# Expert layers of a recurrent and mixture-of-experts kernel: alternating one by one, or in pairs with four activation buffers

## The chip, the cores and the metric

The kernel runs on one core of a Trainium2 chip. The metric is the device time of one execution in microseconds (us); the time before is 6597.48 us, the median of three runs.

## The reference

Input `x` is [4, 4096, 512], float32 throughout. After a layer norm `xn`, two branches meet:

```python
# branch 1, a recurrence over every second token (2048 steps), state h [4, 512, 64]
xz = rms_norm(xn[:, ::2]) @ w_in.T + b_in ; x_proj, gate = split(xz)
h = tanh(h * A + x_t[:, :, None] * Bm)           # one step
y = h @ c_sum + Dv * x_t
s = repeat((y * silu(gate)) @ w_out.T + b_out, 2)
# branch 2, a mixture of experts over every token: H=1024, M=64, E=8, EH=512, top 2
cont = sigmoid(xn @ W_enc + b_enc) @ W_s2c + b_s2c            # [tokens, 64]
probs = softmax(cont @ Wr + br); gate = top-2 weights, normalised, zero elsewhere
hid = relu(cont @ W1[e] + b1[e]) ; y_e = hid @ W2[e] + b2[e]  # for each of 8 experts
decoded = sigmoid((sum_e gate_e * y_e) @ W_c2s + b_c2s) @ W_dec + b_dec
out = x + s * silu(layer_norm(decoded))
```

## The kernel before

The sequence is cut into 64 blocks of 32 recurrence steps (64 tokens of each of 4 batches, 256 tokens a block). All 8 experts are computed for all tokens; the gate scales their input (`conte`, cont times gate, with the gate itself as a 65th row that carries the bias), so that their outputs simply add up in PSUM.

**The recurrence** is done in `step` and `tanh`: 128 partitions hold batch and half of the states, two halves `f` lie in the free dimension. In a step GpSimd (POOL) makes `u = x * Bm` (L499), VectorE (DVE) two products `ps_z = h * A` (L991) and two sums `ps_z += u` (L997), ScalarE (ACT) two tanh (L601). `u` has two buffers: POOL may be one step ahead. Every four steps TensorE (PE) reads `h` for `y` (L761); `h` is a ring of 8 steps, so tanh of step 20 waits for the `y` of steps 12 to 15.

**Everything else** is hung between the steps by hand. The tables at the top give each piece a slot, counted in steps of its block: `ACT_RELU = (13.5, 13.5, 14.5, 14.5, 15.5, ...)` means that ACT does the first two ReLUs after the first tanh of step 13. Negative slots are in the block before, slots of 32 and more in the block after. Each engine runs its own list in order; semaphores join them. Each engine's program is: block 0, a loop of 31 rounds with two blocks each, block 63.

What PE does in a block, in its order, from the experts on:

- `experts` rounds 0 to 16. Round n does `expert_up(n)` (L845: two matmuls of 65 rows and 128 columns of weights over 256 tokens into `bank[n % 2]`, the two halves of one PSUM bank) and then `expert_down(n - 1)` (L857: two matmuls with 64 columns of weights, into the lower and upper half of `ps_acc`). ACT's `relu(n)` (L682) lies between: it takes the bank to `hT[:, n % 2]`. Up n waits until relu n - 2 has freed the bank, down n until relu n is there. The biases of the second layer are one matmul (L853) before the first down. Two calls of `y` are laid between.
- `to_spikes` (L879), `y`, `decode` (L900, two times 8 matmuls of 512 columns, and a one-row bias matmul L892 each), `y`, `encode` of the next block (L794), two `y` and one more.
- `controller` (L806, 64-column weights, result `contT` in `ps_acc`), `fin_transpose` (L912), `router`, `fin_out` (L919 and L921) for the block before, the transposes of the next input (L772), `proj_in` (L781), `y`, the transposes of `conte` (L833), and then the experts.

`router` does, for each of two halves of the tokens, three matmuls: the bias row `br` (one row, L815), cont times `w_r` with 8 columns (L816), and cont times an identity with 64 columns, which transposes it (L817). `logits_copy` (L651), `route` on DVE and `scale_cont` (L665) read them in `ps_acc`.

Around it: DVE's `dec_stats` (L1061) waits for decode, `fin_mul` (L1098, L1099) for `fin_out`; POOL's `fin_skip` (L551) writes into `o`, which is the first part of `conte`'s memory.

Of the kernel before, what the change touches and what calls it, by code (L numbers as in the profile page):

```python
# [23 lines left out]
ACT = mybir.ActivationFunctionType  # L24
AX = mybir.AxisListType

P = 128
# [12 lines left out]
KH = H // P  # L40
M = 64
MA = M + 1
E = 8
EH = 512
T2 = 2 * P
# [6 lines left out]
FILL_ENC, FILL_FIN, FILL_XT, FILL_WIN, FILL_CONTE, FILL_W1, FILL_C2S, FILL_DEC = 0, 4, 6, 8, 10, 14, 30, 33  # L52
# [36 lines left out]
PE_ROUTER = 8  # L89
PE_CONTET = (17, 17, 18, 18)  # L90
PE_GATET = 18
PE_EXPERTS = (19, 19, 19, 19, 19, 19, 19, 19, 19, 19, 19, 20, 22, 22, 24, 28, 28)
PE_TO_SPIKES = (31, 31, 31, 31)
PE_DECODE = (33, 33)
PE_FIN_TRANSPOSE = 39
# [14 lines left out]
def build(nc, x, w_inT, b_in, A_T, B_T, Cm, Dv, w_outT, b_out, g_norm, W_enc, b_enc, W_s2c, b_s2c,  # L110
# [12 lines left out]
    with ExitStack() as ctx:  # L123
        def sb(name, shape):
            return ctx.enter_context(nc.sbuf_tensor(name, shape, F32))
# [9 lines left out]
        w_out = sb("w_out", [P, KD, D])  # L135
        w_enc = sb("w_enc", [P, KD, H])
        w_s2c = sb("w_s2c", [P, KH, M])
        w_r = sb("w_r", [P, E])
        w_1 = sb("w_1", [P, E, EH])
        w_2 = sb("w_2", [P, E * EH // P, M])  # L140
        w_c2s = sb("w_c2s", [P, H])
# [2 lines left out]
        bias_rows = sb("bias_rows", [P, D])  # L144
        ones = sb("ones", [P, P])
# [6 lines left out]
        g_col = sb("g_col", [P, KD])  # L152
        cont_bias = sb("cont_bias", [P, 1])
        ident = sb("ident", [P, P])
        ident_2 = sb("ident_2", [P, M])
        before = sb("before", [P, E, E])
        c_wide = sb("c_wide", [P, F, 2 * SP - 4])
        minus_half = sb("minus_half", [P, 2])
# [15 lines left out]
        hT = sb("hT", [P, 2, 2 * T2])  # L174
# [15 lines left out]
        eoT = hT[:, 0, 0:T2]  # L190
        contT = hT[:, 1, 0:T2]
        gateT = w_1[96:96 + E, 0, 0:T2]
        bias_2 = w_1[96:96 + E, 1, 0:M]
        conteT = wide[0:MA, :, :].rearrange("p (e) t -> p e t", e=E)
        conte_flat = conte[:, :, :, :].rearrange("p q e m -> p (q e m)")
        o = conte_flat[:, 0:D]
        oT = conte_flat[:, D:2 * D].rearrange("p (k t) -> p k t", k=KD)


        ps_A = pb("ps_A", [P, F, D])  # L200
# [2 lines left out]
        bank = [pb("bank0", [P, D]), pb("bank1", [P, D])]  # L203
        ps_acc = pb("ps_acc", [P, D])
        eo_acc = ps_acc[:, 0:T2]
        contT_acc = ps_acc[:, 0:T2]
        gateT_acc = ps_acc[0:E, 0:T2]
        cont_acc = ps_acc[:, T2:T2 + 2 * M].rearrange("p (q m) -> p q m", q=2)
        L0 = T2 + 2 * M
        logit_acc = ps_acc[:, L0:L0 + 2 * E].rearrange("p (q e) -> p q e", q=2)  # L210

        atleast = ps_acc[:, 0:2 * E * E].rearrange("p (q e j) -> p q e j", q=2, e=E)
        rank = ps_acc[:, 128:144].rearrange("p (q e) -> p q e", q=2)
# [40 lines left out]
        eo_ready = sem("eo_ready")  # L254
# [44 lines left out]
        def wait_filled(eng, at):  # L299
            eng.wait_ge(bank_filled[at[1] % 2], count_of(at))  # L300
# [13 lines left out]
        def drained(ins, at):  # L314
            ins.then_inc(bank_drained[at[1] % 2], 1)
# [10 lines left out]
        def wait_dec_drained(eng, blk, q):  # L326
            if q == 0:
                wait_drained(eng, (blk, FILL_DEC))
            else:
                eng.wait_ge(acc_drained, 2 * blk + 2)  # L330
# [42 lines left out]
        def _(sp):  # L373
            def load(dst, src):
                sp.dma_start(dst, src).then_inc(weights_loaded, 16)  # L375
                n_loads[0] += 1
# [54 lines left out]
            load(w_s2c[:, :, :], W_s2c.rearrange("(k p) n -> p k n", p=P))  # L431
            load(bias_rows[0:1, :], b_dec.partition_broadcast(1))
            load(bias_rows[32:33, :], b_out.partition_broadcast(1))
            load(bias_rows[64:65, 0:E], br.partition_broadcast(1))
            load(cont_bias[0:M, :], b_s2c)
            for half in range(2):
                load(w_r[M * half:M * half + M, :], Wr)
            load(w_1[0:M, :, :], W1.rearrange("e m h -> m e h"))
            load(w_1[M:MA, :, :].rearrange("p e h -> p (e h)"), b1.rearrange("e h -> (e h)").partition_broadcast(1))
            load(w_2[:, :, :], W2.rearrange("e (t p) m -> p (e t) m", p=P))  # L440
# [35 lines left out]
        def _(pool):  # L476
# [70 lines left out]
            def fin_skip(blk, par):  # L547


                wait_filled(pool, (blk, FILL_CONTE + 3))  # L550
                pool.tensor_tensor(o, xp[:, par, :], dv_all[:, :], ALU.mult).then_inc(t1_ready, 1)  # L551

            def fin_gate(blk, par):
# [38 lines left out]
        def _(act):  # L592
# [86 lines left out]
            def relu(blk, n):  # L679
                at = (blk, FILL_W1 + n)  # L680
                wait_filled(act, at)
                drained(act.activation(hT[:, n % 2, :], bank[n % 2][:, :], ACT.Relu), at)  # L682

            def eo_copy(blk):
                act.wait_ge(eo_ready, blk + 1)
# [13 lines left out]
            act.wait_ge(pool_made, 8)  # L699
            for half in range(2):  # L700
                rows = slice(M * half, M * half + M)
                act.activation(ident_2[rows, :], ident[rows, rows], ACT.Copy)
            act.activation(ps_A[:, 0, :], h[:, 0, 0, :], ACT.Copy)
            act.activation(ps_A[:, 1, :], h[:, 0, 1, :], ACT.Copy).then_inc(ready, 1)
            proj_norm(0)
# [47 lines left out]
        def _(pe):  # L753
# [44 lines left out]
            def controller(blk):  # L798

                wait_drained(pe, (blk, FILL_ENC + 2))  # L800
                wait_drained(pe, (blk, FILL_ENC + 3))
                if not is_first(blk):
                    wait_dec_drained(pe, blk - 1, 1)
                for k in range(KH):
                    half = k % 2
                    ins = pe.matmul(contT_acc[M * half:M * half + M, :], w_s2c[:, k, :], wide[:, k, :],  # L806
                                    start=(k < 2), stop=(k >= KH - 2))
                ins.then_inc(contT_ready, 1)

            def router(blk):  # L810

                pe.wait_ge(contT_copied, blk + 1)
                for q in range(2):
                    tokens = contT[:, P * q:P * q + P]
                    pe.matmul(logit_acc[:, q, :], ones[64:65, :], bias_rows[64:65, 0:E], start=True, stop=False)  # L815
                    pe.matmul(logit_acc[:, q, :], tokens, w_r[:, :], start=False, stop=True)  # L816
                    ins = pe.matmul(cont_acc[:, q, :], tokens, ident_2[:, :], start=True, stop=True)  # L817
                ins.then_inc(logits_ready, 1)

            def gateT_transpose(blk):  # L820
# [15 lines left out]
            def expert_up(blk, n):  # L836

                at = (blk, FILL_W1 + n)
                e = n // 2
                if n % 4 == 0:  # L840
                    wait_drained(pe, (blk, FILL_CONTE + n // 4))
                wait_free(pe, at)
                for half in range(2):
                    t = 2 * (n % 2) + half
                    ins = pe.matmul(bank[n % 2][:, T2 * half:T2 * half + T2], w_1[0:MA, e, P * t:P * t + P],  # L845
                                    conteT[:, e, :], start=True, stop=True)
                filled(ins, at)

            def expert_down(blk, n):

                if n == 0:
                    pe.wait_ge(gateT_copied, blk + 1)
                    pe.matmul(eo_acc[0:M, :], bias_2, gateT, start=True, stop=False)  # L853
                wait_drained(pe, (blk, FILL_W1 + n))
                for half in range(2):
                    t = 2 * (n % 2) + half
                    ins = pe.matmul(eo_acc[M * half:M * half + M, :], w_2[:, 4 * (n // 2) + t, :],  # L857
                                    hT[:, n % 2, T2 * half:T2 * half + T2],
                                    start=(n == 0 and half == 1), stop=(n == 15))
                if n == 15:  # L860
                    ins.then_inc(eo_ready, 1)

            def experts(blk, n):

                if n < 16:
                    expert_up(blk, n)
                if n > 0:
                    expert_down(blk, n - 1)

            def to_spikes(blk, n):  # L870
                if n == 0:
# [69 lines left out]
            def between(blk, par, slot):  # L941
                for k in range(NQ):
                    if slot == PE_Y[k]:
                        y(blk, k)
                for q in range(2):
                    if slot == PE_PROJ_TRANSPOSE[q]:
                        proj_transpose(blk, q)
                for half in range(2):
                    if slot == PE_PROJ_IN[half]:
                        proj_in(blk, par, half)  # L950
                for n in range(4):
                    if slot == PE_ENCODE[n]:
                        encode(blk, par, n)
                if slot == PE_CONTROLLER:
                    controller(blk)
                if slot == PE_ROUTER:
                    router(blk)
                for n in range(4):
                    if slot == PE_CONTET[n]:
                        conteT_transpose(blk, n)  # L960
                if slot == PE_GATET:
                    gateT_transpose(blk)
                for n in range(17):
                    if slot == PE_EXPERTS[n]:
                        experts(blk, n)
                for n in range(4):
                    if slot == PE_TO_SPIKES[n]:
                        to_spikes(blk, n)
                for q in range(2):
                    if slot == PE_DECODE[q]:  # L970
                        decode(blk, q)
                if slot == PE_FIN_TRANSPOSE:
                    fin_transpose(blk)
                if slot == PE_FIN_OUT:
                    fin_out(blk)
# [5 lines left out]
        def _(dve):  # L981
# [121 lines left out]
            dve.memset(ones[:, :], 1.0)  # L1103
            dve.memset(c_wide[:, :, :], 0.0)
            dve.memset(h[:, RING - 1, :, :], 0.0)
            dve.memset(cont_bias[M:P, :], 0.0).then_inc(consts_made, 1)
            dve.wait_ge(consts_made, 1)
            proj_stats(0)
# [76 lines left out]
```

## Time and profile before

| | us |
|---|---|
| median of 3 runs (6596.17 to 6603.51) | 6597.48 |
| profiled execution, span | 6604.5 |
| PE busy (matmuls) | 6237.1 |
| DVE busy | 5737.4 |
| POOL busy | 5612.7 |
| ACT busy | 3984.4 |

The profile lists an execution of its own; its span is 7.0 us above the median. Busy time of PE has matmuls with modelled ends, so a busy PE may be waiting inside. PEld is the loading of weights, which overlaps. A float32 matmul call stands as two instructions in the trace: x4 in a row is two calls. "issue" means that nothing in the profile explains the wait.

### The profile page before, as it was taken

What the parts mean: (1) busy time and instruction counts of PE and PEld (TensorE: products, weight loads), DVE (VectorE), ACT (ScalarE), POOL (GpSimd) and SP (SyncE); (2) the same over time, 40 slices, a digit from 0 to 9 for tenths busy, and PEclk for the clock granted to TensorE, in tenths of its full rate; (3) what the DMA queues carried; (4) which work ended last, traced back from release to release, by engine and by line L of the source; (5) the groups of instructions that cost most, each with busy time, mean ns of one, the idle gap of its engine ahead of it and who ended that gap; (6) DMA issues with size and microseconds to landing.
All of it is one profiled execution on the core that took longest, in us unless ns stands there. A gap on an engine that the chain in (4) does not pass through costs nothing.

```text
span 6604.5 us, 111352 instructions
## 1 busy us (share of the span) xinstructions
PE 6237.1 (94%) x29376; PEld 3229.9 (49%) x29376; DVE 5737.4 (87%) x10060; ACT 3984.4 (60%) x8390; POOL 5612.7 (85%) x3276
## 2 busy tenths in 40 slices
PE   5999999999999999999999999999999999999998
PEld 3554445445544454454444544445444545444454
DVE  4988889888898888988888888889888898888887
ACT  3666566566565665656656656566566665565665
POOL 4888888888888888888888888888888888888887
PEclk9999999999999999999999999999999999999999
DMA  5443444444444444444344444444444444434443
GB/s 138 104 108 92 104 109 98 106 101 101 105 98 102 100 97 106 103 97 110 93 105 101 100 106 98 103 106 96 105 101 100 106 98 103 106 95 105 103 100 83
DMA packets 158032, 675.52 MB, mean 102 GB/s; under 512 B 45589, under 2 KB 46613, under 8 KB 91799
## 3 DMA queue, kind: packets, MB, share of 16 engines
q1 hardware_dynamic: 157336, 667.24, 41.6%
q8 instruction: 315, 5.16, 0.3%
q14 instruction: 381, 3.12, 0.2%
HBM read 616.73 MB, written 50.33 MB: 101 GB/s over the span
## 4 chain that ended last, share of the span: by engine, by line
POOL 54%; issue 29%; PE 13%; DVE 1%; POOLq 1%; SPq 1%; ACT 1%; DMA 0%; DVEq 0%; ACTq 0%
POOL u L499 46%; PE bank L845 3%; POOL g L545 2%; PE ps_y L761 2%; PE ps_acc L857 2%; PE bank L794 1%; PE bank L781 1%; POOL gt L532 1%; POOL d_r L541 1%; PE bank L900 1%; PE ps_acc L900 1%; POOL conte L551 1%; PE bank L921 1%; POOL p_r L515 1%; SPq L375 1%
## 5 line engine op out<-in xcount | busy, mean ns | idle before, releaser
L499 POOL TENSOR_TENSOR u<-xb,bt 128x1024 f32<-128x1024 f32 x2048 | 4832.9, 2366 | 789.2 <-DVE ps_z L997 782.8
L601 ACT ACTIVATE h<-ps_z 128x512 f32<-128x512 f32 x4096 | 2374.7, 601 | 1691.8 <-DVE ps_z L997 1587.5
L991 DVE TENSOR_TENSOR ps_z<-h,ps_A 128x512 f32<-128x512 f32 x4096 | 2674.1, 691 | 517.3 <-ACT h L601 329.2
L997 DVE TENSOR_TENSOR ps_z<-ps_z,u 128x512 f32<-128x512 f32 x4096 | 2660.7, 691 | 39.6 <-POOL u L499 37.3
L845 PE MATMUL bank<-wide,w 65*128 65x256 f32 x4096 | 1141.2, 404 | 1.9
L761 PE MATMUL ps_y<-h,c_wide 128*32 128x512 f32 x8192 | 1007.1, 610 | 80.4 <-ACT h L601 80.4
L794 PE MATMUL bank<-xnT,w_enc 128*128 128x256 f32 x4096 | 922.4, 384 | 49.5 <-DVE g L1082 42.6
L845 PEld LDWEIGHTS bank<-wide,w 65*128 65x128 f32 x4096 | 700.2, 189 | 449.8 <-issue 320.2
L794 PEld LDWEIGHTS bank<-xnT,w_enc 128*128 128x128 f32 x4096 | 772.4, 191 | 256.9 <-issue 81.0
L682 ACT ACTIVATE hT<-bank 128x512 f32<-128x512 f32 x1024 | 604.0, 598 | 383.8 <-PE bank L845 366.4
L857 PE MATMUL ps_acc<-hT,w 128*64 128x256 f32 x4096 | 668.7, 405 | 6.6
L761 PEld LDWEIGHTS ps_y<-h,c_wide 128*32 128x32 f32 x8192 | 216.3, 110 | 615.2 <-issue 416.3
L900 PE MATMUL bank<-w_dec,wide 128*128 128x512 f32 x1024 | 480.3, 624 | 0.0
L900 PE MATMUL ps_acc<-w_dec,wide 128*128 128x512 f32 x1024 | 456.6, 599 | 0.0
L781 PE MATMUL bank<-w_in,xnT 128*128 128x512 f32 x1024 | 453.9, 597 | 0.0
L857 PEld LDWEIGHTS ps_acc<-hT,w 128*64 128x64 f32 x4096 | 202.5, 134 | 357.2 <-issue 296.8
L900 PEld LDWEIGHTS bank<-w_dec,wide 128*128 128x128 f32 x1024 | 199.1, 200 | 286.4 <-issue 286.4
L900 PEld LDWEIGHTS ps_acc<-w_dec,wide 128*128 128x128 f32 x1024 | 189.7, 190 | 262.4 <-issue 262.4
L921 PE MATMUL bank<-w_out,conte 128*128 128x512 f32 x512 | 313.9, 770 | 0.0
L624 ACT ACTIVATE wide<-bank,b_enc_col 128x256 f32<-128x256 f32 x512 | 213.9, 471 | 148.1 <-PE bank L794 148.1
L781 PEld LDWEIGHTS bank<-w_in,xnT 128*128 128x128 f32 x1024 | 191.4, 192 | 216.8 <-issue 216.5
L665 ACT ACTIVATE conte<-ps_acc,gate 128x64 f32<-128x64 f32 x1024 | 226.5, 369 | 0.0
(107 smaller groups left out, 4324.6 us busy)
## 6 DMA issues: line engine op xcount, KB each, us to landing
xb<-x_proj_scratch SPq DMA_DIRECT2D x2048, 256.0 KB, 4.3
xbuf<-in_L_attn_x SPq DMA_DIRECT2D x256, 128.0 KB
xres<-in_L_attn_x SPq DMA_DIRECT2D x512, 64.0 KB
out<-g SPq DMA_DIRECT2D x256, 128.0 KB
x_proj_scratch<-xp SPq DMA_DIRECT2D x256, 64.0 KB
w_in<-in_L_attn_w_in SPq DMA_DIRECT2D x1, 2048.0 KB
w_enc<-in_L_ffn_W_enc SPq DMA_DIRECT2D x1, 2048.0 KB
w_dec<-in_L_ffn_W_dec SPq DMA_DIRECT2D x1, 2048.0 KB
```

Source lines behind the costliest of these rows:

```text
L499: pool.tensor_tensor(u[:, tau % 2, :, :], xt, bt[:, :, :], ALU.mult).then_inc(u_ready, 1)
L601: act.activation(h[:, tau % RING, f, :], ps_z[:, f, :], ACT.Tanh).then_inc(h_ready, 1)
L682: drained(act.activation(hT[:, n % 2, :], bank[n % 2][:, :], ACT.Relu), at)
L761: ins = pe.matmul(ps_y[32 * j:32 * j + 32, :], c_wide[:, f, SP - 4 - 4 * k:2 * SP - 4 - 4 * k], h[:, (QUAD * k + j) % RING, f, :], start=( ...
L781: ins = pe.matmul(bank[half][:, :], xnT[:, par, k, 0, :], w_in[:, k, D * half:D * half + D], start=(k == 0), stop=(k == KD - 1))
L794: ins = pe.matmul(bank[n % 2][:, T2 * half:T2 * half + T2], w_enc[:, k, P * m:P * m + P], xnT[:, par, k, :, :], start=(k == 0), stop=(k == ...
L845: ins = pe.matmul(bank[n % 2][:, T2 * half:T2 * half + T2], w_1[0:MA, e, P * t:P * t + P], conteT[:, e, :], start=True, stop=True)
L857: ins = pe.matmul(eo_acc[M * half:M * half + M, :], w_2[:, 4 * (n // 2) + t, :], hT[:, n % 2, T2 * half:T2 * half + T2], start=(n == 0 and ...
L900: ins = pe.matmul(dst[:, :], wide[:, k, P * q:P * q + P], w_dec[:, k, :], start=False, stop=(k == KH - 1))
L921: ins = pe.matmul(bank[1][:, :], oT[:, k, :], w_out[:, k, :], start=False, stop=(k == KD - 1))
L991: dve.tensor_tensor(ps_z[:, f, :], h[:, (tau - 1) % RING, f, :], ps_A[:, f, :], ALU.mult).then_inc(m_done, 1)
L997: dve.tensor_tensor(ps_z[:, f, :], ps_z[:, f, :], u[:, tau % 2, f, :], ALU.add).then_inc(z_ready, 1)
```

## The change

- Experts go in pairs: nine rounds, round p does up 2p, up 2p + 1, then down 2p - 2, down 2p - 1. `PE_EXPERTS` has nine slots. ReLU results have four places: the two of `hT`, and two in `conte`'s memory, which nothing reads once it is transposed. ACT's slots are the same.
- POOL's `fin_skip`, which writes into that memory, waits until the last down is done (`eo_ready`) and no longer for the last transpose of `conte`.
- The router has one matmul for each half of the tokens, 72 columns wide: `w_r` and the identity lie side by side. The bias of both halves (144 columns, one row) is put into `ps_acc` by one matmul ahead of the controller's; this one opens the bank, the others accumulate.

```diff
-PE_EXPERTS = (19, 19, 19, 19, 19, 19, 19, 19, 19, 19, 19, 20, 22, 22, 24, 28, 28)
+PE_EXPERTS = (19, 19, 19, 19, 19, 20, 22, 24, 28)
...
-        w_r = sb("w_r", [P, E])
+        w_r = sb("w_r", [P, E + M])
...
+        br_row = w_1[96:97, 2, 0:2 * (E + M)]
...
+        hidden = [hT[:, 0, :], hT[:, 1, :], conte_flat[:, 0:2 * T2], conte_flat[:, 2 * T2:4 * T2]]
...
+        routed = ps_acc[:, T2:T2 + 2 * (E + M)].rearrange("p (q n) -> p q n", q=2)
+        logit_acc = routed[:, :, 0:E]
+        cont_acc = routed[:, :, E:E + M]
...
-                wait_filled(pool, (blk, FILL_CONTE + 3))
+                pool.wait_ge(eo_ready, blk + 1)
...
-                drained(act.activation(hT[:, n % 2, :], bank[n % 2][:, :], ACT.Relu), at)
+                drained(act.activation(hidden[n % 4], bank[n % 2][:, :], ACT.Relu), at)
...
+                pe.matmul(ps_acc[:, T2:T2 + 2 * (E + M)], ones[96:97, :], br_row, start=True, stop=True)
                 for k in range(KH):
                     half = k % 2
                     ins = pe.matmul(contT_acc[M * half:M * half + M, :], w_s2c[:, k, :], wide[:, k, :],
-                                    start=(k < 2), stop=(k >= KH - 2))
+                                    start=False, stop=(k >= KH - 2), skip_group_check=True)
...
-                    pe.matmul(logit_acc[:, q, :], ones[64:65, :], bias_rows[64:65, 0:E], start=True, stop=False)
-                    pe.matmul(logit_acc[:, q, :], tokens, w_r[:, :], start=False, stop=True)
-                    ins = pe.matmul(cont_acc[:, q, :], tokens, ident_2[:, :], start=True, stop=True)
+                    ins = pe.matmul(routed[:, q, :], tokens, w_r[:, :], start=False, stop=True,
+                                    skip_group_check=True)
...
-                                    hT[:, n % 2, T2 * half:T2 * half + T2],
+                                    hidden[n % 4][:, T2 * half:T2 * half + T2],
...
-            def experts(blk, n):
+            def experts(blk, p):
 
-                if n < 16:
-                    expert_up(blk, n)
-                if n > 0:
-                    expert_down(blk, n - 1)
+                if p < 8:
+                    expert_up(blk, 2 * p)
+                    expert_up(blk, 2 * p + 1)
+                if p > 0:
+                    expert_down(blk, 2 * p - 2)
+                    expert_down(blk, 2 * p - 1)
```

PE at the start of the experts, in the loop, before (`wide` holds the transposed `conte`, `w` is `w_1` or `w_2`):

```order
L845 MATMUL bank<-wide,w 128x256 x4
L853 MATMUL ps_acc<-w 64x256
L303 REGISTER_ALU
L857 MATMUL ps_acc<-hT,w 64x256 x2
L845 MATMUL bank<-wide,w 128x256 x2
L857 MATMUL ps_acc<-hT,w 64x256 x2
L845 MATMUL bank<-wide,w 128x256 x2
```

and in the change:

```order
L848 MATMUL bank<-wide,w 128x256 x4
L310 REGISTER_ALU
L848 MATMUL bank<-wide,w 128x256 x4
L856 MATMUL ps_acc<-w 64x256
L860 MATMUL ps_acc<-hT,w 64x256 x4
L310 REGISTER_ALU
L848 MATMUL bank<-wide,w 128x256 x4
L860 MATMUL ps_acc<-conte,w 64x256 x4
```

A run of ups or downs is now twice as long; the first down comes after four ups and no longer after two.

PE around the router, in the loop, before:

```order
L806 MATMUL ps_acc<-wide,w_s2c 64x256 x8
L912 MATMUL bank<-ident,conte 128x128 x4
L812 REGISTER_ALU
L815 MATMUL ps_acc<-bias_rows,ones 128x8
L816 MATMUL ps_acc<-w_r,hT 128x8
L817 MATMUL ps_acc<-ident,hT 128x64
L815 MATMUL ps_acc<-bias_rows,ones 128x8
L816 MATMUL ps_acc<-w_r,hT 128x8
L817 MATMUL ps_acc<-ident,hT 128x64
L303 REGISTER_ALU
L919 MATMUL bank<-bias_rows,ones 128x512
```

and in the change:

```order
L807 MATMUL ps_acc<-w,ones 128x144
L810 MATMUL ps_acc<-wide,w_s2c 64x256 x8
L917 MATMUL bank<-ident,conte 128x128 x4
L816 REGISTER_ALU
L819 MATMUL ps_acc<-w_r,hT 128x72 x2
L304 REGISTER_ALU
L924 MATMUL bank<-bias_rows,ones 128x512
```

Six small calls have become two, and one call with a single row stands ahead of the controller.

## Rows read from the trace of the kernel before

**Rows 1.** The profile's page, part 1: busy us, share, instructions.
```profile
PE 6237.1 (94%) x29376; PEld 3229.9 (49%) x29376; DVE 5737.4 (87%) x10060; ACT 3984.4 (60%) x8390; POOL 5612.7 (85%) x3276
```

**Rows 2.** Line L686, once a block: ns min/median/max, first and last start.
```profile
L686 ACT ACTIVATE hT<-ps_acc x64: 404/405/408, 155.5 to 6552.7; 128x256 f32<-128x256 f32 x64
```

**Rows 3.** Timeline of PE, experts of one block: start, length (us), times, idle before.
```profile
3070.99 2.00 PE L845 MATMUL bank<-wide,w 65*128 65x256 f32 x8
3072.91 0.64 PE L853 MATMUL ps_acc<-w 8*64 8x256 f32 x2
3073.49 0.65 PE L857 MATMUL ps_acc<-hT,w 128*64 128x256 f32 x4
3074.07 1.13 PE L845 MATMUL bank<-wide,w 65*128 65x256 f32 x4
3075.13 0.65 PE L857 MATMUL ps_acc<-hT,w 128*64 128x256 f32 x4
...
3098.35 1.41 PE L857 MATMUL ps_acc<-hT,w 128*64 128x256 f32 x8
3099.68 1.92 PE L761 MATMUL ps_y<-h,c_wide 128*32 128x512 f32 x16
```

**Rows 4.** Timeline of ACT, experts of that block.
```profile
3080.17 0.60 ACT L682 ACTIVATE hT<-bank 128x512 f32<-128x512 f32 x1 [1.05 <-PE bank L845]
3080.66 1.08 ACT L601 ACTIVATE h<-ps_z 128x512 f32<-128x512 f32 x2
3081.81 0.60 ACT L682 ACTIVATE hT<-bank 128x512 f32<-128x512 f32 x1
```

**Rows 5.** Timeline of DVE: two steps among the experts, two after them.
```profile
3081.28 1.29 DVE L991 TENSOR_TENSOR ps_z<-h,ps_A 128x512 f32<-128x512 f32 x2 [0.79 <-ACT h L601]
3084.57 1.29 DVE L991 TENSOR_TENSOR ps_z<-h,ps_A 128x512 f32<-128x512 f32 x2 [0.79 <-ACT h L601]
...
3104.77 1.29 DVE L991 TENSOR_TENSOR ps_z<-h,ps_A 128x512 f32<-128x512 f32 x2
3107.32 1.29 DVE L991 TENSOR_TENSOR ps_z<-h,ps_A 128x512 f32<-128x512 f32 x2
```

**Rows 6.** Busy time by stretch: length, PE, PEld, DVE, ACT, POOL, granted clock, DMA.
```profile
3080.00:3101.00 21.00, 20.90 (x118) 9.99 (x120) 16.98 (x28) 14.01 (x26) 17.22 (x8) 1.00 0.28 66
3101.00:3143.00 42.00, 42.00 (x188) 23.17 (x180) 40.67 (x68) 24.22 (x48) 40.30 (x24) 1.00 0.54 137
...
3149.60:3153.00 3.40, 3.40 (x5) 1.33 (x4) 2.86 (x8) 2.65 (x5) 3.40 (x3) 0.50 0.49 104
```

**Rows 7.** Timeline of all engines around the router.
```profile
3143.05 1.95 PE L806 MATMUL ps_acc<-wide,w_s2c 128*64 128x256 f32 x16
3145.57 0.38 PE L815 MATMUL ps_acc<-bias_rows,ones 1*128 1x8 f32 x2
3145.88 0.39 PE L816 MATMUL ps_acc<-w_r,hT 128*128 128x8 f32 x2
3145.89 0.60 ACT L696 ACTIVATE conte<-bank 128x512 f32<-128x512 f32 x1
3146.12 0.41 PE L817 MATMUL ps_acc<-ident,hT 128*128 128x64 f32 x2
3147.37 1.12 PE L919 MATMUL bank<-bias_rows,ones 1*128 1x512 f32 x2
3151.48 1.27 POOL L545 TENSOR_TENSOR g<-g,sg 128x512 f32<-128x512 f32 x1
3153.95 0.69 DVE L1098 TENSOR_TENSOR g<-bank,g 128x512 f32<-128x512 f32 x1 [1.46 <-PE bank L921]
```

**Rows 8.** Timeline, the next block, where the loop's round ends.
```profile
3205.48 1.93 PE L761 MATMUL ps_y<-h,c_wide 128*32 128x512 f32 x16 [2.33 <-ACT h L601]
3228.97 1.29 DVE L991 TENSOR_TENSOR ps_z<-h,ps_A 128x512 f32<-128x512 f32 x2 [4.12 <-issue]
```

**Rows 9.** Spans and granted clock.
```profile
core 0: 6604.5 us, clock 0.975
```

More of the change, by code:

```diff
@@ L154, in build @@
         ident = sb("ident", [P, P])
-        ident_2 = sb("ident_2", [P, M])
         before = sb("before", [P, E, E])
@@ L207, in build @@
         gateT_acc = ps_acc[0:E, 0:T2]
-        cont_acc = ps_acc[:, T2:T2 + 2 * M].rearrange("p (q m) -> p q m", q=2)
-        L0 = T2 + 2 * M
-        logit_acc = ps_acc[:, L0:L0 + 2 * E].rearrange("p (q e) -> p q e", q=2)
+        routed = ps_acc[:, T2:T2 + 2 * (E + M)].rearrange("p (q n) -> p q n", q=2)
+        logit_acc = routed[:, :, 0:E]
+        cont_acc = routed[:, :, E:E + M]
         atleast = ps_acc[:, 0:2 * E * E].rearrange("p (q e j) -> p q e j", q=2, e=E)
@@ L433, in _ @@
             load(bias_rows[32:33, :], b_out.partition_broadcast(1))
-            load(bias_rows[64:65, 0:E], br.partition_broadcast(1))
+            for q in range(2):
+                load(br_row[:, (E + M) * q:(E + M) * q + E], br.partition_broadcast(1))
             load(cont_bias[0:M, :], b_s2c)
             for half in range(2):
-                load(w_r[M * half:M * half + M, :], Wr)
+                load(w_r[M * half:M * half + M, 0:E], Wr)
             load(w_1[0:M, :, :], W1.rearrange("e m h -> m e h"))
@@ L701, in _ @@
                 rows = slice(M * half, M * half + M)
-                act.activation(ident_2[rows, :], ident[rows, rows], ACT.Copy)
+                act.activation(w_r[rows, E:E + M], ident[rows, rows], ACT.Copy)
             act.activation(ps_A[:, 0, :], h[:, 0, 0, :], ACT.Copy)
@@ L962, in between @@
                     gateT_transpose(blk)
-                for n in range(17):
+                for n in range(9):
                     if slot == PE_EXPERTS[n]:
@@ L1105, in _ @@
             dve.memset(h[:, RING - 1, :, :], 0.0)
+            for q in range(2):
+                dve.memset(br_row[:, (E + M) * q + E:(E + M) * (q + 1)], 0.0)
             dve.memset(cont_bias[M:P, :], 0.0).then_inc(consts_made, 1)
```

## The prediction

> **What bounds the kernel now.** I read the page's busy times first, then one block in the timelines, engine by engine. PE is busy 94% of the span, DVE 87%, POOL 85% [rows 1], so three engines could bound it and only the waits in a block can tell which does where. One line that runs once a block starts first at 155.5 and last at 6552.7, 64 times [rows 2]: 6397.2 / 63 = 101.5 us a block. What a block saves is saved 64 times.
>
> The stretches of one block show two kinds of time [rows 6]. From 3080 to 3101, among the experts, PE is busy 20.90 of 21.00, while DVE is busy 16.98 and POOL 17.22: **PE leads here**, and the others idle some 4 us. How they hang on it is seen in ACT's and DVE's rows. ACT's ReLU waits 1.05 for the up matmul, and only behind it comes the next tanh [rows 4]; DVE's products wait 0.79 for that tanh, and one step follows the other after 84.57 - 81.28 = 3.29 us, against 107.32 - 104.77 = 2.55 after the experts [rows 5]. 3.29 is two expert rounds of PE: an up takes 3075.13 - 3074.07 = 1.06 and a down 3074.07 - 3073.49 = 0.58, so a round takes 1.64 [rows 3].
>
> From 3101 to 3143 PE is busy 42.00 of 42.00, DVE 40.67 and POOL 40.30 [rows 6]: all three are nearly full. Nothing in the change shortens this stretch; it can only begin earlier. Then comes the router's stretch, in which DVE's `fin_mul` waits 1.46 for `fin_out` [rows 7], partly because PE runs at a granted clock of 0.50, the 1.2 GHz level, from 3149.6 to 3153.0 [rows 6]. At the end of a loop round DVE stands 4.12 and PE 2.33 [rows 8]; it is the loop's branch, the change leaves it alone, and it falls on every second block.
>
> **The experts in pairs.** Before, PE needs 3099.68 - 3070.99 = 28.69 us from the first up to the second `y` [rows 3]. It adds up: two ups in a row 1.92, bias 0.58, 14 single ups at 1.06, 14 single downs at 0.58, the last two downs 1.33 (they wait for a ReLU), one `y` of 1.86 (its 1.92 less the overlap), together 28.65. What a repeated shape costs stands in two rows. Two ups in a row are 2.00 long and one is 1.13, so the second costs 0.87 and not 1.06 [rows 3]. Four pairs of 64-column matmuls side by side, the controller's, are 1.95 long [rows 7], and one such pair, a down, is 0.65 [rows 3]: each further pair costs 0.43 and not 0.58. So a change of shape from up to down and back costs 0.19 + 0.15 = 0.34 us, and the change takes away about half of these.
>
> After: 8 double ups at 1.92 are 15.36, 8 double downs at 0.58 + 0.43 = 1.01 are 8.08, bias 0.58, `y` 1.86: 25.88. That is **2.81 less a block**. The double down is what no row shows undisturbed. Its bounds: 1.01 as above, and 1.33, the only two downs in a row [rows 3], with which the gain is 28.69 - (15.36 + 10.64 + 0.58 + 1.86) = 0.25. I take 1.01, since the controller's matmuls have the same shape (128 rows, 64 columns, 256 tokens) and no ReLU between them.
>
> Do the others follow? A group of two ups and two downs takes 1.92 + 1.01 = 2.93 us, still above the 2.55 that a step needs without waits, so PE keeps the lead and DVE gains with it. ACT has two ReLUs and two tanh in it, 0.60 + 0.60 + 1.08 = 2.3 us [rows 4], which fits. The first ReLU of a group can start about 1 us after the ups begin, and its bank is needed again after 2.93, so a pair of tanh (1.08) can come in between with some 0.3 us to spare; the four places free the second ReLU from waiting for a down. DVE's and POOL's idle 4 us among the experts hold 2.8. The tanh of step 20, which waits for the first `y` in this stretch, gets it earlier too, since six groups lie ahead of it instead of twelve rounds.
>
> **The router.** Six calls take 3147.37 - 3145.57 = 1.80, 0.30 each; two remain, 0.60. The new one-row call ahead of the controller is bounded by the one-row call with 8 columns, 0.31 from start to start, and the bias row of `fin_out` with 512, 1.12 long [rows 7]; by columns it lies at about 0.5. I take 0.5. So PE would save 0.7. But `fin_out` also waits for ACT's L696, which starts at 3145.89 and lasts 0.60; it moves back by the same 0.5 with the controller, to 3146.99, so `fin_out` starts at about 3147.04 instead of 3147.37: 0.33 us. Behind it POOL's L545 ends at 3152.75, and `fin_mul` needs it; so at most 3153.95 - 3152.75 = 1.2 us can be gained here, even with a full clock [rows 7]. Where PE isn't late (blocks with full clock here), the gain is 0. I take 0.2 a block, with 0 and 1.2 as ends. The ACT copy of `contT` and the tanh behind it come 0.5 later; DVE is then busy with two other instructions, so I cost this at nothing; without that cover it would be up to 0.5 a block.
>
> **Smaller parts.** POOL's `fin_skip` stands in slot 31, some 20 us after the last down: the new wait costs nothing. ACT, DVE, POOL and SP have the same instructions in the loop. The setup has two small loads and two memsets more, under the large weight loads: nothing.
>
> **Sum.** 2.8 + 0.2 = 3.0 us a block, 64 blocks: 192. The profiled execution spans 6604.5, so 6412; its span lies 7 above the median, so **6405 us**.
>
> **Rivals.**
> 1. *Half of it is lost.* ReLUs come in pairs right behind a double up, and a tanh pair comes between them; if each group waits 0.2 us for ACT, a block loses 8 x 0.2 = 1.6, and the time is 6405 + 102 = 6507. For it speaks the narrow margin of 0.3 us above, and that DVE, POOL and PE are all nearly full after the experts, so that a gain must reach all three; against it, that ACT is idle 7.0 of 21.0 us in this stretch [rows 6].
> 2. *Repeating a shape saves nothing.* The 0.19 and 0.15 belong to the loading of weights and not to the change of shape; they would show in every call. Then only the router is left, 0.2 x 64 = 13 us: about 6585, and with the ACT delay of the router uncovered 6597. The rows speak against it: the second of two ups is cheaper by 0.19, though its weights are loaded too. The Trainium skill (TensorE: Matmul & The Clock Gate, Part 3, "What overlaps and what doesn't") says that weights load beside a running matmul only when the row group differs; up and down both use all row groups here, so by it grouping would bring nothing. The trace disagrees so far, by that second up of 0.87.
> 3. *Slower: PE's clock.* The mean granted clock is 0.975 [rows 9], so some 5% of the span, 330 us, are at 1.2 GHz, 5.2 us a block. They come after stretches in which PE had small calls (the router) or stood at the loop's end [rows 6, 8]. With a shorter program PE waits more often for DVE; if the low clock came to cover `decode` in every block, each us at 1.2 GHz costs half a us. To eat 3.0 us a block it needs 6.0 us more of it, more than twice as much as now; with 8 us more the time is 6405 + 64 x 4 = 6661. Against it: the change removes small calls and puts in no wait where PE leads. The Trainium skill (same page, "Why this matters for your kernels") warns of idle gaps between bursts of matmuls; here PE has one gap of 2.33 in two blocks, as before.
>
> **How the numbers follow.** About 0.2% is what a measurement of this kernel can tell from no change, 13 us. The forecast, 6350 to 6465, has 0.73; rival 1 (6465 to 6584) 0.18; rival 2 0.05; rival 3 0.04. Faster 0.91, same 0.05, slower 0.04. The low end is reached with 2.8 + 1.2 a block, 256 us: 6341; the high end with half of the experts' gain, 1.4 a block: 6508. The clock may shift either by some 30 us. I give 6345 to 6505.
>
> **What would show it.** In the profile after: double ups start to start 1.92 and double downs 1.01; from first up to second `y` 25.9 instead of 28.7; steps among the experts 2.93 apart; L686 98.5 apart on average. The router's two calls take 0.6, the new bias call 0.5. I am wrong if groups take 3.3 (rival 2), if PE rows among the experts show waits for ACT (rival 1), or if the mean clock falls below 0.95 (rival 3).

## The result, and the profile after

The change is slower: 6787.2 us median of 4 runs (6752.29 to 6834.85) against 6598.35, a ratio of 1.0288 with a 95% interval of 1.0244 to 1.0332. The forecast was 6405, faster. Of `pairs_only` and `start_then_singles` further down, two of four executions each ran over 1.5% above the fastest of the same kernel, and their times and ratios below leave these out. PE's new rows came out as forecast and the time did not, so the clock is the first thing to look at. Three lines of the page of the changed kernel (the span, the busy times, the granted clock in 40 slices), and its mean clock:

```profile
span 6833.1 us, 110339 instructions
...
PE 6389.3 (94%) x28992; PEld 3440.5 (50%) x28992; DVE 5740.9 (84%) x10062; ACT 3987.0 (58%) x8390; POOL 5613.7 (82%) x3276
...
PEclk9998889998899899899799998898989999989988
```

```profile
core 0: 6833.1 us, clock 0.919
```

PE is busy 152 us longer than in [rows 1], with 384 instructions fewer, and the mean granted clock fell from 0.975 [rows 9] to 0.919. The trace shows where: in 28 of 64 blocks it falls to 0.50, the 1.2 GHz level, 3.1 to 5.4 us after the first up (the first matmul of the experts), and it is back only 24 to 31 us later, 806 us in all. Before the change it never fell there. One such block by stretches (columns as in [rows 6]):

```profile
690.00:731.00 41.00, 38.59 (x188) 21.70 (x190) 40.15 (x78) 25.07 (x62) 39.63 (x30) 1.00 0.46 109
731.00:739.10 8.10, 7.58 (x53) 4.37 (x46) 7.50 (x13) 6.60 (x13) 6.85 (x3) 1.00 0.31 66
739.10:769.80 30.70, 30.70 (x96) 16.17 (x94) 15.71 (x26) 11.95 (x22) 17.93 (x9) 0.50 0.30 69
```

In the last one PE is busy 30.70 of 30.70 us and still gets 1.2 GHz, while DVE is busy only half of the time. The timeline of PE there, which answers to [rows 3]:

```profile
735.88 1.99 PE L848 MATMUL bank<-wide,w 65*128 65x256 f32 x8
738.36 3.08 PE L848 MATMUL bank<-wide,w 65*128 65x256 f32 x8 [0.49 <-ACT hT L684]
741.37 1.11 PE L856 MATMUL ps_acc<-w 8*64 8x256 f32 x2
742.41 1.98 PE L860 MATMUL ps_acc<-hT,w 128*64 128x256 f32 x8
744.31 3.78 PE L848 MATMUL bank<-wide,w 65*128 65x256 f32 x8
748.02 1.97 PE L860 MATMUL ps_acc<-conte,w 128*64 128x256 f32 x8
...
766.78 3.41 PE L763 MATMUL ps_y<-h,c_wide 128*32 128x512 f32 x16
770.12 1.99 PE L848 MATMUL bank<-wide,w 65*128 65x256 f32 x8
```

A double up is 1.99 long at full clock and 3.78 at the low one. Two things were not in the forecast. PE **stands still for 0.49 us before the third up**, and the low clock holds until `y` (L763) comes. Why it stands still is in ACT's timeline:

```profile
736.73 1.09 ACT L603 ACTIVATE h<-ps_z 128x512 f32<-128x512 f32 x2
737.70 1.09 ACT L684 ACTIVATE hT<-bank 128x512 f32<-128x512 f32 x2
```

The third up needs the bank that ReLU 0 frees. ReLU 0 has its slot behind the second tanh of step 13 (slot 13.5 means that, and not behind the first tanh, as the section on the kernel before has it). It starts at 737.70 and ends about 738.3; PE goes on at 738.36. Before the change ReLU 0 came at the same place, 1.82 us after the first up of [rows 3]:

```profile
3071.84 1.09 ACT L601 ACTIVATE h<-ps_z 128x512 f32<-128x512 f32 x2
3072.81 1.10 ACT L682 ACTIVATE hT<-bank 128x512 f32<-128x512 f32 x2
```

It ended about 3073.4, while the bias matmul ran from 3072.91; the first down followed at 3073.49 and the third up at 3074.07, so no wait was seen.

### The profile page after: what moved, and what is told of

Same layout as the page of the kernel before. It is cut to its first block, busy times and chain, and to the rows that moved or that the text cites. A ratio compares the mean times of both kernels' runs of the same rounds, so it can differ in the third digit from the quotient of the medians.

```text
span 6833.1 us, 110339 instructions
## 1 busy us (share of the span) xinstructions
PE 6389.3 (94%) x28992; PEld 3440.5 (50%) x28992; DVE 5740.9 (84%) x10062; ACT 3987.0 (58%) x8390; POOL 5613.7 (82%) x3276
## 4 chain that ended last, share of the span: by engine, by line
POOL 51%; issue 31%; PE 13%; DVE 2%; ACT 2%; POOLq 1%; SPq 1%; DMA 0%; DVEq 0%; ACTq 0%
POOL u L501 43%; PE bank L848 3%; PE ps_y L763 2%; POOL g L547 2%; PE ps_acc L860 2%; PE bank L783 2%; POOL gt L534 1%; DVE ps_z L1002 1%; ACT h L603 1%; PE bank L796 1%; POOL d_r L543 1%; POOL conte L553 1%; DVE ps_z L996 1%; POOL g L566 1%; POOL conte L557 1%
## 5 line engine op out<-in xcount | busy, mean ns | idle before, releaser
L848 PE MATMUL bank<-wide,w 65*128 65x256 f32 x4096 | 1235.4, 453 | 33.0 <-ACT hT L684 31.0
L763 PE MATMUL ps_y<-h,c_wide 128*32 128x512 f32 x8192 | 1035.8, 625 | 93.8 <-ACT h L603 93.8
L848 PEld LDWEIGHTS bank<-wide,w 65*128 65x128 f32 x4096 | 864.3, 222 | 438.3 <-issue 234.9
L763 PEld LDWEIGHTS ps_y<-h,c_wide 128*32 128x32 f32 x8192 | 219.9, 112 | 655.7 <-issue 453.8
L783 PE MATMUL bank<-w_in,xnT 128*128 128x512 f32 x1024 | 479.3, 623 | 0.0
L684 ACT ACTIVATE hT<-bank 128x512 f32<-128x512 f32 x512 | 299.7, 601 | 260.9 <-PE bank L848 260.9
L684 ACT ACTIVATE conte<-bank 128x512 f32<-128x512 f32 x512 | 292.6, 597 | 213.1 <-PE bank L848 209.4
L860 PE MATMUL ps_acc<-hT,w 128*64 128x256 f32 x2048 | 349.6, 473 | 0.0
L860 PE MATMUL ps_acc<-conte,w 128*64 128x256 f32 x2048 | 324.1, 444 | 0.0
L926 PE MATMUL bank<-w_out,conte 128*128 128x512 f32 x512 | 268.4, 673 | 0.0
```

The costliest lines, as they stand in the source:

```text
L684: drained(act.activation(hidden[n % 4], bank[n % 2][:, :], ACT.Relu), at)
L763: ins = pe.matmul(ps_y[32 * j:32 * j + 32, :], c_wide[:, f, SP - 4 - 4 * k:2 * SP - 4 - 4 * k], h[:, (QUAD * k + j) % RING, f, :], start=( ...
L783: ins = pe.matmul(bank[half][:, :], xnT[:, par, k, 0, :], w_in[:, k, D * half:D * half + D], start=(k == 0), stop=(k == KD - 1))
L926: ins = pe.matmul(bank[1][:, :], oT[:, k, :], w_out[:, k, :], start=False, stop=(k == KD - 1))
```

## The experiments

Three theories for the falls: (A) the start with four ups in a row causes them; (B) pairs anywhere do; (C) the router's part does. A was later split in two: (A1) the standstill, or four ups with nothing between them; (A2) the late first down. A fourth, (D), came later too: the clock falls, and stays low, because ups use only 65 of the 128 rows of the array. "Falls" below means falls of the clock among the experts, counted in one profiled execution of 64 blocks. Times are medians, and ratios are to the kernel before, run on the same chip, where it took 6606 to 6610 us.

**pairs_only** and **router_only**: each half of the change alone.

> Experts in pairs, router as before. Seen after the change: in 27 of 64 blocks the granted clock falls to 0.5 some 3 to 5 us after the first up and stays there for 27 to 31 us. If the pairs cause it (theory A: the start with four ups; theory B: pairs anywhere), the time stays near that of the change, 6740 to 6860, mean clock about 0.92, with falls among the experts. If the router's part causes it (theory C, by shifting where low activity falls), the time is near 6420 and the clock 0.97.

> Router with one matmul per half, experts one by one as before. Theories A and B: 6575 to 6600 (the 0 to 0.33 us a block of the prediction), no fall of the clock among the experts. Theory C: 6700 or more, falls among the experts.

`pairs_only` took 6786 us (ratio 1.0267, 1.0235 to 1.0299) with 23 falls; `router_only` 6566.16 (0.9937, 0.9918 to 0.9957) with none. Theory C is out. The router's part is a gain by itself, 0.6%, and more than I expected (6575 to 6600). By the medians it is 40 us, 0.63 us a block, about three times the 0.2 that I took for it; by the interval of the ratio 0.4 to 0.85. The clock goes with it: the four executions run from 6556.58 at a mean clock of 0.982 to 6584.32 at 0.977. In the profiled one, the fastest, the low stretches from the controller's first matmul to the next block's first up sum to 133 us; in the profile before they sum to 181.

**start_then_singles** and **singles_then_pairs**: the order of the experts, written out (u is up, d down, b the bias).

```diff
-PE_EXPERTS = (19, 19, 19, 19, 19, 20, 22, 24, 28)
+# start_then_singles
+EXPERT_ROUNDS = ('u0 u1', 'u2 u3 b d0 d1', 'u4 d2', 'u5 d3', ..., 'u15 d13', 'd14 d15')
+# singles_then_pairs
+EXPERT_ROUNDS = ('u0', 'u1 b d0', 'u2 d1', 'u3 d2', 'u4 u5 d3', 'u6 u7 d4 d5', ..., 'u14 u15 d12 d13', 'd14 d15')
```

> The change, but only its first four ups in a row; after the first two downs ups and downs alternate one by one. Theory A (the start makes the clock fall): falls 3 to 5 us after the first up as in the change; how long they last tells whether alternating gets the clock back (short, about 10 us) or whether nothing in the experts does (27 us and more, up to the next y). Theory B (pairs anywhere): falls gone or at another place, 6590 to 6620. Theory A gives 6700 to 6900.

> The change, but ups 0 to 3 and downs 0 to 2 one by one as before, pairs from up 4 on. Theory A: no fall among the experts, since the start is as before; six of eight groups keep the gain of 0.34 us each, some 2 us a block: 6440 to 6500. Theory B: falls later among the experts, 6600 to 6850.

`start_then_singles` took 6845 us (1.0356, 1.0324 to 1.0388), within theory A's range. The execution that was profiled took 7013.97 and has 30 falls at the same place, 3.1 to 5.5 us after the first up. The two executions behind the 6845 have mean clocks of 0.937 and 0.932, which fits falls there too, fewer of them. So the start is enough. And alternating does not get the clock back: the falls last 27 to 34 us, up to `y`. One such block of that profile, the low stretch and what follows:

```profile
2027.80:2058.50 30.70, 30.70 (x87) 14.30 (x90) 15.53 (x25) 12.07 (x22) 16.49 (x9) 0.50 0.31 69
2058.50:2068.90 10.40, 10.40 (x68) 4.61 (x60) 7.12 (x12) 5.92 (x12) 5.97 (x3) 1.00 0.16 45
```

`singles_then_pairs` took 6497.72 us (0.9827, 0.9811 to 0.9843), no falls. Theory A holds, B is out: six double ups kept the full clock in all 64 blocks.

**What in the start it is.** Three edits of the change:

```diff
+# bias_between
+EXPERT_ROUNDS = ('u0 u1', 'b u2 u3 d0 d1', 'u4 u5 d2 d3', ..., 'd14 d15')
+# relu_earlier
-ACT_RELU = (13.5, 13.5, 14.5, ...)
+ACT_RELU = (13, 13.5, 14.5, ...)
+# two_singles
+EXPERT_ROUNDS = ('u0', 'u1 b d0', 'u2 u3 d1', 'u4 u5 d2 d3', ..., 'd14 d15')
```

> The change, with the bias matmul (0.58 us) between the second and the third up instead of behind the fourth. In the change PE stands still 0.49 us there, waiting for the first ReLU. Theory A1 (it is the standstill, or four 65-row ups with nothing between): no falls of the clock among the experts, 6400 to 6470. Theory A2 (it is how late the first down comes, still behind four ups, 4.4 us after the first): falls in about as many blocks as after the change, 6740 to 6860.

> The change, with the first ReLU before the second tanh of step 13 instead of behind it. The order on PE is that of the change, only the standstill before the third up shrinks from 0.49 to 0.1 us or less. Theory A1, by the standstill alone: no falls, 6400 to 6470. Theory A2, or if four ups in a row are enough by themselves: falls stay, 6730 to 6850.

> The change, with up 0, up 1, bias, down 0 as before, and pairs right from up 2. The first 4 us then hold four ups and two downs instead of four ups. Theory A2: few or no falls, and up to 0.7 us a block more than with three single rounds: 6440 to 6500. If falls come back here (6600 or more), two single rounds are too few and the stretch that matters is longer.

`relu_earlier` took 6449.48 us (0.9755, 0.9736 to 0.9775), no falls. PE does the same instructions in the same order as after the change; the standstill is down to 0.07 us (the third up starts 1.99 us after the first, where a double up takes 1.92; in the change 2.48):

```profile
3094.13 4.10 PE L848 MATMUL bank<-wide,w 65*128 65x256 f32 x16
3098.16 0.64 PE L856 MATMUL ps_acc<-w 8*64 8x256 f32 x2
3098.73 1.08 PE L860 MATMUL ps_acc<-hT,w 128*64 128x256 f32 x8
3099.75 1.99 PE L848 MATMUL bank<-wide,w 65*128 65x256 f32 x8
...
3120.09 1.92 PE L763 MATMUL ps_y<-h,c_wide 128*32 128x512 f32 x16
```

So four ups in a row are not enough by themselves: **in this order of PE the clock falls in 28 of 64 blocks with the 0.49 us of standstill, and in none without it**. `bias_between` took 6485.09 us (0.9809, 0.9761 to 0.9857; two executions, 6458.49 and 6511.69, at mean clocks of 0.970 and 0.960). It has no standstill either, but a matmul of 8 rows and 64 columns in its place, and 9 falls are left of the 28. That is neither of my two expectations: falls come without a standstill too, if a small matmul stands there, though fewer. `two_singles` took 6451.91 (0.9759, 0.9739 to 0.9778), no falls: the bias and one down of 128 rows before the third up are enough. Its time fell in the range of theory A2, but `relu_earlier`, where the first down is as late as in the change, rules A2 out as the cause by itself.

**rows128**: the same start, standstill included, but more of the array at work. The 63 rows that are added have zero weights; the data under them are not zero, they are what `wide` still holds of the encoder's sigmoid. The small tables that lay in these rows of `w_1` have a tile of their own (not shown).

```diff
-                    ins = pe.matmul(bank[n % 2][...], w_1[0:MA, e, P * t:P * t + P], conteT[:, e, :], ...)
+                    ins = pe.matmul(bank[n % 2][...], w_1[:, e, P * t:P * t + P], conteT_all[:, e, :], ...)
+            dve.memset(w_1[M:P, :, :], 0.0).then_inc(w_1_cleared, 1)
```

> The change, with all ups over 128 rows instead of 65: the 63 rows added have zero weights, so the result is the same and each matmul takes the same time; the small tables that lay in the unused rows have a tile of their own. Theory D (what lets the clock fall, and keeps it low for 27 us and more although PE is never idle, is that ups use only half of the rows): no falls, or short ones; 6390 to 6470. If rows do not matter, falls as after the change, 6740 to 6860.

6505.3 us (0.9838, 0.9804 to 0.9873), and no falls. The standstill is there, the durations are the same:

```profile
2418.60 1.99 PE L852 MATMUL bank<-wide,w 128*128 128x256 f32 x8
2421.08 1.99 PE L852 MATMUL bank<-wide,w 128*128 128x256 f32 x8 [0.49 <-ACT hT L688]
```

The falls are gone as theory D has it, but the time lies above my range of 6390 to 6470. That range was made with the forecast's 3.0 us a block, and `relu_earlier` shows that 2.5 were to be had; the rest of the miss stays open (see the next section).

**rows128_late**: 65 rows in ups 0 to 3, 128 from up 4 on (`w_1[0:P if n > 3 else MA, ...]`). This lets the falls come and asks how long they last.

> The change with ups 0 to 3 over 65 rows as in it, and ups 4 to 15 over 128 rows (63 of them with zero weights). The start, and so the falls of the clock 3 to 5 us after the first up, should be those of the change (in 20 to 30 of 64 blocks). If the clock then stays low because ups with half of the rows are too little for it to rise (theory D), it comes back within some 3 to 10 us instead of 27 to 31, and the time is 6500 to 6620. If rows play no part in that, it stays low up to the y behind six groups, 27 us, and the time is 6700 or more.

6561.57 us (0.9926, 0.9906 to 0.9946). 27 falls, at 3.1 to 5.5 us as after the change, but each lasts 3.4 or 6.8 us, and 109 us in all instead of 806. One of them, by stretches and in PE's timeline:

```profile
2137.00:2140.40 3.40, 3.40 (x12) 1.99 (x9) 3.34 (x7) 1.60 (x3) 3.21 (x2) 0.50 0.95 217
2140.40:2160.00 19.60, 19.60 (x121) 11.81 (x123) 15.71 (x26) 13.91 (x26) 15.89 (x9) 1.00 0.25 57
```

```profile
2134.31 1.99 PE L852 MATMUL bank<-wide,w 65*128 65x256 f32 x8 [0.48 <-ACT hT L688]
2136.23 0.64 PE L860 MATMUL ps_acc<-extra 8*64 8x256 f32 x2
2136.80 1.84 PE L864 MATMUL ps_acc<-hT,w 128*64 128x256 f32 x8
2138.57 2.88 PE L852 MATMUL bank<-wide,w 128*128 128x256 f32 x8
2141.38 1.08 PE L864 MATMUL ps_acc<-conte,w 128*64 128x256 f32 x8
```

PE is busy all the time in these stretches of both kernels. The one difference is the number of rows from up 4 on, and in all 27 blocks the clock is back 1.4 to 2.4 us after up 4 starts, within the first double up of 128 rows. The longer falls are those that began earlier. So the rows matter for both, falling and staying down. They aren't the cause alone: the kernel before has 65 rows and no falls. It takes rows and standstill together, or the small matmul of `bias_between`.

**Both cures**, and the best order:

> Both cures at once: all ups over 128 rows, and the first ReLU one tanh earlier (no standstill of 0.49 us before the third up). Each alone removed the falls among the experts. If the clock was all that they mended, both together are as fast as the earlier ReLU alone, 6430 to 6460; the standstill itself is worth 0.4 x 64 = 26 us against 128 rows alone (6505).

> Two single rounds first (which removed the falls, 6452) and the first ReLU one tanh earlier. There is no standstill left to remove; if the order of PE alone counts, 6445 to 6465, and no falls among the experts.

`rows128_relu_earlier` took 6460.58 us (0.9766, 0.9744 to 0.9787), not apart from the earlier ReLU alone (the expected range ended at 6460), which fits that padding mends nothing but the clock. `two_singles_relu_earlier` took **6447.6 us (0.9752, 0.9733 to 0.9771)**, no falls. It, `relu_earlier` and `two_singles` can't be told apart; each beats the kernel before by 2.4 to 2.5% and the change by some 5%.

## Why the prediction was wrong

**What bounds the kernel: right before the change, not after it.** PE leads among the experts, and where the falls are gone DVE's idle time behind ACT's tanh sinks as PE's stretch gets shorter, from 329 us before to 160 in `relu_earlier`. The waits of the two kernels (us in total, times, longest), and two steps among the experts of `relu_earlier`:

```profile
DVE ps_z L991 <- ACT h L601: 329.2, 571, 2.3
```

```profile
DVE ps_z L996 <- ACT h L603: 160.5, 327, 2.7
```

```profile
3103.75 1.29 DVE L996 TENSOR_TENSOR ps_z<-h,ps_A 128x512 f32<-128x512 f32 x2
3106.31 1.29 DVE L996 TENSOR_TENSOR ps_z<-h,ps_A 128x512 f32<-128x512 f32 x2
```

But the prediction had PE keep the lead, with steps 2.93 apart. They are 2.56 apart, the 2.55 that a step takes without waits: with PE's groups at 2.94, DVE no longer hangs on PE here and has nothing more to gain. Nor was 3.29 the rule before: over blocks 2 to 60 the steps among the experts were 2.97 apart on average, and are 2.71 in `relu_earlier`. Ten steps of a block start there, so this is 2.6 us a block, about all that it gains.

**The price of the pairs: right.** At full clock and without the standstill the span from first up to second `y` is 3120.09 - 3094.13 = 25.96 us in `relu_earlier`; 25.88 was forecast, 28.69 it was [rows 3]. Double ups start to start are 1.92 and double downs 1.02; 1.92 and 1.01 were forecast. The choice of the controller's row over the 1.33 of the only double down was the right one. Rival 2 is out: grouping does save. So is what it drew from the Trainium skill (TensorE: Matmul & The Clock Gate, Part 3, "What overlaps and what doesn't"), by which grouping would bring nothing.

**"Which fits": the step that failed.** I worked out that ReLU and tanh of a group fit into 2.93 us, and that the bank is needed again 2.93 us after the ups begin. That is so from the second group on. In the first group no down stands between the ups, so the bank is needed after 1.92 us, and ReLU 0, behind two tanh, ends at 2.4. The wait was to be had from the order of PE, in which four ups stand in a row, and from where ReLU 0 stands before the change. By itself it costs little: from first up to `to_spikes` `rows128` takes 28.19 us and `relu_earlier` 27.82, and 0.37 x 64 = 24 us. Rival 1 had this wait, 0.2 us in every group; it came in the first group alone. What it sets off costs far more.

**The clock: the right rival, with the wrong mechanism and a chance of 0.04.** Rival 3 had a lower clock turning the gain into a loss, but sought it in `decode`, after waits for DVE. It came among the experts, where PE leads, with a mean clock of 0.919, below the 0.95 that was named as its sign. `rows128` has the same order and the same standstill and no falls: its span is 6496.1, that of the change 6833.1. The 28 falls cost the difference, 337 us, **12 us each** (an estimate from one profiled execution of either kernel; the change was profiled in the slowest of its four). A block with a fall takes 41.92 us from first up to `to_spikes` on average, 42.84 at worst, instead of 28.19. That is 384 us for all 28. The rest of the blocks is some 0.8 us shorter than in `rows128`, which makes up the difference; why was not tested. The span forecast was 6604.5 - 192, and 337 on top of it leaves 84 us of the 6833.1 unexplained.

Of these, 24 are the standstill. Another 31 are seen in `relu_earlier`, without falls or standstill: it spans 6443.8, a gain of 161 us, 2.5 a block and not 3.0. Its PE is busy 6032.9, 204 less than before, but idle 44 us more: in front of the input transposes for DVE, and in front of `y` and `fin_out` for ACT. The steps "so PE keeps the lead and DVE gains with it" and "it can only begin earlier" took DVE and POOL to pass on all of PE's gain. The experts did get 2.73 us shorter (30.55 to 27.82), but the rest of the block (again over blocks 2 to 60) took 71.5 us against 71.3 before, though the router's part alone had brought it to 70.5. The last 28 or so lie between `relu_earlier` and `rows128`; the second has 399 us at 1.2 GHz and the first 358, worth up to 20 us at half a us each, and executions of `rows128` lie up to 47 us apart. No run separates this.

**The router: under-sized.** 0.2 us a block was forecast, 0.6 measured alone, still within the ends of 0 and 1.2. The new bias call started the controller's matmuls 0.43 us later (0.5 was forecast), the two calls of the router are 0.67 long, and `fin_out` waits for ACT as forecast. It starts 3.93 us after the first of these rows, where it was 4.32 after the controller's first matmul [rows 7], 0.39 sooner; 0.33 was forecast:

```profile
2417.70 0.51 PE L807 MATMUL ps_acc<-w,ones 1*128 1x144 f32 x2
2418.13 1.95 PE L810 MATMUL ps_acc<-wide,w_s2c 128*64 128x256 f32 x16
2420.01 0.66 PE L917 MATMUL bank<-ident,conte 128*128 128x128 f32 x4
2420.66 0.67 PE L819 MATMUL ps_acc<-w_r,hT 128*128 128x72 f32 x4
2421.63 1.12 PE L924 MATMUL bank<-bias_rows,ones 1*128 1x512 f32 x2 [0.31 <-ACT conte L698]
```

So the step was about right in this block, and the 0.2 for the mean over blocks was too low. The low clock around it also got shorter; how much of the gain that is was not separated.

## What to carry to other kernels

When matmuls are regrouped, follow the first group by hand through every buffer: the steady groups can all fit while the first one stalls. And before forecasting a gain on a PE that leads, look at how much of the array each stretch uses, in rows as well as in time: here a stretch of half-filled matmuls kept the full clock, and a standstill of 0.49 us near its start cost it in 28 of 64 blocks, at some 12 us each. Padding the contraction with zero weights took no time on PE here (1.99 us a double up with 65 rows or 128) and removed the falls, where the memory is there and the data under the zero weights are finite. Last, price a gain by the engine that leads after the change: beyond the point where the next one is full, it isn't passed on.

## What the runs showed of the hardware

- A PE that is busy without a gap does not get its full clock back by that. It was busy 30.70 of 30.70 us at 0.50 with ups of 65 rows and downs of 64 columns, whether in pairs or one by one, and its full clock returned 0.4 to 4.5 us after the start of the first `y` (128 rows, four column tiles at a time) or, in `rows128_late`, 1.4 to 2.4 us after the first up of 128 rows. The Trainium skill (TensorE: Matmul & The Clock Gate, Part 1, "What's actually happening") says that activity releases the throttle. Here PE had matmuls in flight for 30.70 us and the throttle stayed, so that in this stretch the trace does not agree if activity is read as being busy.
- Rows with zero weights were enough here: the 63 added rows were zero in all weights, with data that were not zero, and the 28 falls became none. Data of zero were not tried.
- The same half-filled stretch kept the full clock through all of the experts in every block that passed the first 6 us without a fall. Why a fall comes in some blocks and not in others of the same program (28 of 64) was not tested.
